# An attention layer's end rows joined in five groups of tiles, and duplicate edges counted against near keys only, in a four-network graph kernel on one core

## The reference

```python
edge_index = jnp.stack([src, dst])
x = _layernorm(x + _L0_gnn_ref(x, edge_index, W, att_src, att_dst, bias), axis=-1)   # attention, 8 heads
x = _layernorm(x + _L1_gnn_ref(x, edge_index, w0a, b0a, w0b, b0b, ...), axis=-1)     # 3 x sum of neighbours and two dense layers
x = _layernorm(x + _L2_gnn_ref(x, edge_index, W, att_src, att_dst, ...), axis=-1)    # attention, 4 heads, with a skip product
x = _layernorm(x + _L3_gnn_ref(x, edge_index, edge_weight, W1, b1, ...), axis=-1)    # 3 x weighted sum of neighbours
```

```python
alpha = leaky_relu(a_src[src] + a_dst[dst], 0.2)
alpha = exp(alpha - segment_max(alpha, dst)[dst])
out = segment_sum(x[src] * (alpha / (segment_sum(alpha, dst)[dst] + EPS))[:, :, None], dst)
```

## Time and profile before

| | |
|---|---|
| time of three runs, us | 7126.04 median (7118.27 to 7150.4) |
| time of the profiled execution, us | 7125.99 |
| its span, us | 7124.2 |
| DVE busy | 3269.2 us, 46% of the span |
| POOL busy | 3459.4 us, 49% |
| PE (TensorE) busy | 3212.4 us, 45% |
| first scatter (L593, `plane<-begun,cell`) | 782 instructions, 831.9 us busy, 338.9 us idle before them |
| duplicate count (L556) | 782 instructions, 756.8 us busy, 211.4 us idle before them |
| span of the first scatter | 1363.4 to 2533.9 us |

### The profile page before, as it was taken

The page is one execution under the profiler, slowest core; times in us unless marked ns, Lnnn a source line. Parts: engine busy times, 40 slices in busy tenths (PEclk is TensorE's granted clock), DMA queues, the critical chain, the costliest instruction groups (busy, mean ns, idle before and its releaser), DMA issues. The chain is left out here.

```text
span 7124.2 us, 38615 instructions
## 1 busy us (share of the span) xinstructions
PE 3212.4 (45%) x11661; PEld 2005.2 (28%) x11661; DVE 3269.2 (46%) x5638; ACT 1783.3 (25%) x1855; POOL 3459.4 (49%) x3338
## 2 busy tenths in 40 slices
PE   3000000000000079999999500000015999999999
PEld 2000000000000057777778400000013444544544
DVE  5565555698687723445657344444446000000111
ACT  1233333100000056666667322222210000000000
POOL 3677777677667755556667277777730000000000
PEclk8555555555555589999999755555557999999999
DMA  3355555209950056433358333333323888888887
GB/s 108 137 206 172 188 175 185 93 0 329 372 219 0 0 174 210 151 106 111 111 163 251 122 99 110 98 106 102 102 70 104 284 293 294 288 293 294 294 299 261
DMA packets 502441, 1242.14 MB, mean 174 GB/s; under 512 B 114227, under 2 KB 162841, under 8 KB 493273
## 3 DMA queue, kind: packets, MB, share of 16 engines
q1 hardware_dynamic: 382408, 1114.01, 45.8%
q0 software_dynamic: 119824, 125.65, 7.4%
HBM read 861.79 MB, written 377.50 MB: 174 GB/s over the span
## 5 line engine op out<-in xcount | busy, mean ns | idle before, releaser
L361 POOL DMA_INDIRECT gb<-rows,src x1564 | 1589.8, 1017 | 679.0 <-issue 548.5
L754 PE MATMUL psum<-gb,big 128*128 128x512 f32 (+1 forms) x3822 | 1579.3, 568 | 3.0 <-DVE gb L778 2.0
L593 POOL DMA_INDIRECT plane<-total,cell x782 | 836.4, 1070 | 558.0 <-DVE gb L574 192.9
L1108 ACT CAST strips<-gb 128x1024 fp32r<-128x1024 f16 (+1 forms) x764 | 805.1, 1077 | 1068.2 <-DMA gb<-plane 913.9
L1820 PE MATMUL psum<-identity,end_top 128*8 128x128 f32 (+1 forms) x2 | 0.8, 375 | 2277.6 <-issue 1173.9
L593 POOL DMA_INDIRECT plane<-begun,cell x782 | 831.9, 1064 | 338.9 <-issue 236.1
L1091 PE MATMUL psum<-strips,high 128*128 128x512 f32 (+1 forms) x1274 | 398.9, 401 | 1269.1 <-DVE strips L778 1252.9
L754 PEld LDWEIGHTS psum<-gb,big 128*128 128x128 f32 x3822 | 691.5, 190 | 770.9 <-issue 770.9
L556 DVE SCALAR_TENSOR_TENSOR psum<-gb,psum 128x782 f32<-128x782 f32 x782 | 756.8, 1032 | 211.4 <-remote 136.6
L1820 PEld LDWEIGHTS psum<-identity,end_top 128*8 128x8 f32 (+1 forms) x2 | 0.2, 82 | 2278.3 <-issue 1174.3
L1805 ACT COPY gb<-turned 128x1632 f32<-128x1632 f32 (+3 forms) x138 | 450.7, 3266 | 727.6 <-DVE turned L1893 514.6
(11 more groups left out here) (305 smaller groups left out, 3754.9 us busy)
## 6 DMA issues: line engine op xcount, KB each, us to landing
gb<-plane SPq DMA_DIRECT2D x588, 512.0 KB, 4.5
gb<-plane SPq DMA_DIRECT2D x294, 576.0 KB, 4.8
plane<-turned SPq DMA_DIRECT2D x49, 3200.0 KB
gb<-plane SPq DMA_DIRECT2D x588, 256.0 KB
gb<-plane SPq DMA_DIRECT2D x294, 288.0 KB
plane<-turned SPq DMA_DIRECT2D x49, 1600.0 KB
runs<-gb SPq DMA_DIRECT2D x33, 1748.0 KB
runs<-gb SPq DMA_DIRECT2D x33, 1610.0 KB
```

The costliest lines, as they stand in the source:

```text
L361: m.s_rows[b % BUFS].up(nc.gpsimd.indirect_dma_start(m.batch(b, columns, row)[:, j, 0:width], None, table, bass.IndirectOffsetOnAxis(ap=m. ...
L593: done.up(m.nc.gpsimd.indirect_dma_start(plane, bass.IndirectOffsetOnAxis(ap=m.cell[:, r:r + 1], axis=0), total[:, r:r + 1], None), 16)
L754: mm = nc.tensor.matmul(m.psum[:, self.bank(r, 0, i), 0:nodes], rows, slot[:, a:a + nodes], start=(s == 0), stop=False)
L1108: m.s_strip_act.up(nc.scalar.copy(out, landed))
```

## The change

Two parts.

**Near keys.** `count_edges` compares column `r` of group `b` with the first `near = min(COLS, (b + 3) * 23)` columns alone. The width of the instruction grows by 23 with every group, from 69 in group 0 to 782 from group 31 on. The number of instructions stays.

**Groups of end rows.** The 49 tiles are taken as 12, 12, 12, 12 and 1 (three quads, then what is left). DVE waits for the quads of one group, makes its factors, and then scales and adds the rows of the group before it; the last group's rows come at the end. ACT's two exponentials become five pairs.

```diff
@@ count_edges
+        near = min(COLS, (b + BUFS) * NARROW)
         for r in range(b * NARROW, (b + 1) * NARROW):
             if r > 1:
                 dve.wait_ge(m.s_compared.sem, r - 1)
             m.s_compared.up(nc.vector.scalar_tensor_tensor(
-                m.unread[r % 2], m.key, m.key[:, r:r + 1], m.step[:, COLS - 1 - r:2 * COLS - 1 - r], ALU.is_equal, ALU.mult,
+                m.unread[r % 2][:, 0:near], m.key[:, 0:near], m.key[:, r:r + 1], m.step[:, COLS - 1 - r:COLS - 1 - r + near], ALU.is_equal, ALU.mult,
                 accum_out=m.total[:, r:r + 1]))
+def end_groups():
+    return [slice(t, min(t + 3 * QUAD, TILES)) for t in range(0, TILES, 3 * QUAD)]
@@ attention_layer, ACT
-            act.wait_ge(m.s_logits.sem, m.s_logits.at(batches + 3))
-            m.s_probs.up(nc.scalar.activation(a, a, ACT.Exp))
-            m.s_probs.up(nc.scalar.activation(b_, b_, ACT.Exp))
+            for n, t in enumerate(end_groups()):
+                act.wait_ge(m.s_logits.sem, m.s_logits.at(batches + 3 + n))
+                m.s_probs.up(nc.scalar.activation(a[:, t, :], a[:, t, :], ACT.Exp))
+                m.s_probs.up(nc.scalar.activation(b_[:, t, :], b_[:, t, :], ACT.Exp))
@@ attention_layer, DVE
-            for g in range(QUADS):
-                dve.wait_ge(m.s_end[g].sem, m.s_end[g].at(16 * len(tiles_of(g))))
...
+            def factors(t):
+                node_top, own_top = ends[:, t, S:S + H], own[:, t, S:S + H]
+                for g in range(t.start // QUAD, -(-t.stop // QUAD)):
+                    dve.wait_ge(m.s_end[g].sem, m.s_end[g].at(16 * len(tiles_of(g))))
...
+            def add(n, t):
+                size = t.stop - t.start
+                many = [P, size, H, C + 1]
+                dve.wait_ge(m.s_probs.sem, m.s_probs.at(batches + 2 + 2 * (n + 1)))
...
+            groups = end_groups()
+            for n, t in enumerate(groups):
+                factors(t)
+                if n:
+                    add(n - 1, groups[n - 1])
...
+            add(len(groups) - 1, groups[-1])
```

More of the change, by code:

```diff
@@ L1934, in _ @@
                 count_edges(m, dve, 0, COUNTED_BEFORE)
-            for g in range(QUADS):
-                dve.wait_ge(m.s_end[g].sem, m.s_end[g].at(16 * len(tiles_of(g))))
+            def factors(t):
+                node_top, own_top = ends[:, t, S:S + H], own[:, t, S:S + H]
+                for g in range(t.start // QUAD, -(-t.stop // QUAD)):
+                    dve.wait_ge(m.s_end[g].sem, m.s_end[g].at(16 * len(tiles_of(g))))
+                c.link(nc.vector.tensor_tensor(own_top, node_top, b_[:, t, :], ALU.max))
+                c.link(nc.vector.tensor_tensor(a[:, t, :], node_top, own_top, ALU.subtract))
+                c.link(nc.vector.tensor_scalar(a[:, t, :], a[:, t, :], LOW, None, ALU.max))
+                m.s_logits.up(nc.vector.tensor_tensor(b_[:, t, :], b_[:, t, :], own_top, ALU.subtract))
@@ new lines, in add @@
+            def add(n, t):
+                size = t.stop - t.start
+                many = [P, size, H, C + 1]
+                dve.wait_ge(m.s_probs.sem, m.s_probs.at(batches + 2 + 2 * (n + 1)))
+                c.start(nc.vector.tensor_tensor(split(ends_sum[:, t, :]), split(ends_sum[:, t, :]),
+                                                a[:, t, :].unsqueeze(3).broadcast_to(many), ALU.mult))
+                c.link(nc.vector.tensor_tensor(split(own_sum[:, t, :]), split(own_sum[:, t, :]),
+                                               b_[:, t, :].unsqueeze(3).broadcast_to(many), ALU.mult))
+                c.link(nc.vector.tensor_tensor(own_sum[:, t, :], own_sum[:, t, :], ends_sum[:, t, :], ALU.add))
@@ L1937, in _ @@
+            groups = end_groups()
[3 more added lines that the diff above has]
+                    add(n - 1, groups[n - 1])
             if head.first:
                 c.start(nc.vector.tensor_scalar(m.dinv[:, :], ends[:, :, S + H], 1.0, None, ALU.add))
-            node_top = ends[:, :, S:S + H]
-            c.link(nc.vector.tensor_tensor(own[:, :, S:S + H], node_top, b_, ALU.max))
-            c.link(nc.vector.tensor_tensor(a, node_top, own[:, :, S:S + H], ALU.subtract))
@@ L1942, in _ @@
-            c.link(nc.vector.tensor_scalar(a, a, LOW, None, ALU.max))
-            m.s_logits.up(nc.vector.tensor_tensor(b_, b_, own[:, :, S:S + H], ALU.subtract))
-            dve.wait_ge(m.s_probs.sem, m.s_probs.at(batches + 4))
-            many = [P, TILES, H, C + 1]
-            c.link(nc.vector.tensor_tensor(split(ends_sum), split(ends_sum), a.unsqueeze(3).broadcast_to(many), ALU.mult))
-            c.link(nc.vector.tensor_tensor(split(own_sum), split(own_sum), b_.unsqueeze(3).broadcast_to(many), ALU.mult))
@@ L1948, in _ @@
-            c.link(nc.vector.tensor_tensor(own_sum, own_sum, ends_sum, ALU.add))
+            add(len(groups) - 1, groups[-1])
     m.settle()
```

## The result

The changed kernel takes 7100.29 us (median of 14 executions, 7089.84 to 7114.79), the kernel before 7117.34 (median of 14, 7086.16 to 7163.68). The ratio is 0.9965, its 95% interval 0.9951 to 0.9979: 25 us less, 14 to 35 by the interval. The gain is real, but smaller than the 0.5% that was named as the bound of no change. The forecast was 7009 in a range from 6988 to 7045, with a chance of 0.94 for more than 0.5%: wrong, since most of the gain it saw didn't come. The profiled executions show 7125.99 before and 7089.84 after, 36 us; the time is followed in these two.

The account below looks back on a forecast made before the run. The prediction took POOL's scatter to end the stage, with DVE counting only where POOL waits. It summed -16.8 - 94.2 - 6 = -117 against the profiled 7125.99 to 7009 us, range 6988 to 7045.

Parts of the forecast that it names:

- What bounds the kernel: First scatter's stage: POOL, not DVE, ends it; DVE counts only where POOL waits for it, 102.2 us in 12 waits.
- The start of group 2's scatter: First layer: POOL starts group 2's scatter at 1431.5 instead of 1448.3 without stopping, -16.8 us, including 7.98 of waiting.
- The second layer: Second attention layer's end: joining end rows in groups saves 10.3 us, gathers and factors cost 4.4; net -6 us.
- The waits behind it: From group 2's scatter on: POOL's remaining 94.2 us of waits for DVE's cells all go if DVE stays ahead.
- 23% of the counts stay at 2.8 us: DVE's groups 8 to 33: slow share stays 23% of 598 counts, so 724 us are needed, done at 2278.
- The worst bound: DVE's groups 8 to 33: rate unchanged at 1.51, then 1.34 us a count, done at 2400; POOL loses 6 us.
- a starved start: Rival, 14%: a slow stretch falls into group 2, some 16 counts at 2.8 us; POOL waits 33 us, time 7042.
- POOL's 1.27 us: First layer's scatter from group 2 on: POOL needs 1.27 us a scatter, 29.3 us a group, reaching the last group at 2394.
- The rival on the other side: Slower than before, 2%: DVE's supply of instructions bounds the counts; 40% slow counts gives the old end, 50% gives 7240.
- The place where I said I would look: DVE's slow stretches: instruction fetch not fully hidden may explain them, and blocks used up sooner could make them worse.
- The two that didn't: Slower than before, counts bound by DVE's instruction supply (2%, 7240 us); nothing gained, width doesn't set a count's cost (3%, 7120).

Follow-up runs that it names:

- before_again: The kernel before, unchanged, run and traced once more at the 7100 level: 7147.43 us (one execution; 7157.51 the median of 23 in this set).
- after_again: The whole change, unchanged, run and traced once more beside the kernel before at the 7100 level: 7131.91 us, ratio 0.9968.
- batched: The change with a group's 23 counts made in three DVE instructions over the keys of five groups: 7107.53 us, ratio 0.9947 of the kernel before.
- batched_fill_2: Three-instruction counts per group plus 200 unused DVE comparisons behind the last count, against the change: 7085.44 us at 7100; 6790.8 us, 0.9965, at 6815.
- one_more_4: The change with a one-column memset added to each count from group 2 on: 7142.7 us at 7100; 6793.43 (0.9968), 6793.51 and 6791.58 us at 6815.
- near_only: The kernel before with near keys and no groups of end rows, at the 6815 level: 6807.37, 6804.61 and 6807.53 us, ratios 0.9989, 0.9986, 0.9989.
- groups_only: The change with full-width counts put back, so groups of end rows alone, at the 6815 level: 6801.18 and 6800.3 us, ratio 0.998 in both.

## Why the prediction was wrong, point by point

**What bounds the kernel: right.** POOL's scatter ends the stage in both kernels, and its end moved SP's load with it.

**The start of group 2's scatter, -16.8: right.** It measured -14.6 (1433.76, forecast 1431.5), with no wait. The joins of 1.85 us beside the scatters cost POOL a little more than one scatter of 1.85 for each. The scatters took 2.65, 1.45 and 1.58 us beside the first three, and the gathers ahead ended 6.2 us later than before.

**The second layer, -6: right**, at -5.8. The part at the end measured 11.1 us (25.6 to 14.5), forecast 10.3; the gathers paid 5.3, forecast 4.4. Beside a join's three instructions of 1.80 us the timeline has gathers of 2.49, 1.41 and 1.54 us in place of 0.95. The lock between DVE and POOL of which the Trainium skill's page "SBUF — State Buffer", section "SBUF: two separate sides", speaks is there; but one POOL instruction passes for each of DVE's, as the forecast took it from the rows.

**The waits behind it, -94.2: this is the step that failed.** It measured -6.9; in the second pair of traces, before_again and after_again, it was -1.2 (17.3 us at group 2's start, 18.5 at the last scatter). In the prediction's words, "They go if DVE stays ahead", and "both ends of this unknown leave at least 88 of the 94.2, and I take all of it". Three things in that step were wrong.

1. *23% of the counts stay at 2.8 us.* The share of slow counts was read as a property that would carry over. It depends on POOL's waits: a slow stretch lasts until POOL stops, and POOL stops when it has used up DVE's lead. With faster counts between the stretches the lead is larger, POOL takes longer to use it up, and the stretch goes on for more counts. So 17, 17, 18, 17, 29, 17 and 9 counts a stretch became 38, 37, 39, 24, 23, 24 and 23 in the first pair of traces. DVE's pace from group 8 on went from 32.5 us a group to 31.3, and in the second pair from 32.3 to 32.8. What the faster counts gained between the stretches was given back in them. What begins a stretch, no run shows.
2. *The worst bound.* It had this very case, "its rate stays what it was", at 1.51 and 1.34 us a count. The rate was 1.41 for groups 8 to 20 and 1.31 behind them, near the bound. But the bound was started from a lead of 91 us, with group 7 done at 1554. A slow stretch of 94 us (1439.1 to 1532.7) lay in groups 4 and 5, so group 7 came at 1633.5. The rival "a starved start" had this, but at 16 counts and with fast counts behind it. Each was priced as if the other didn't occur, though both are the same mechanism. Together they are 6 + 80 = 86 us lost, 7009 + 86 = 7095; 7100 was measured. That this comes so close is partly luck. The bound compares only the ends, and there DVE was ahead: its last cells came at 2447, and POOL began that group at 2483. What POOL lost it lost in the waits on the way.
3. *POOL's 1.27 us.* The prediction took POOL's pitch as free of everything once the waits were gone. At 7100 POOL comes down to 1.40 in the two kernels without waits, some 290 us behind the SELU stage's wide instructions (batched, batched_fill_2). So even with all waits gone POOL takes 1050 us from group 2's first scatter (1433.9) to the last (2484.1), where the forecast had 991. The term was too large by 59 us even for a kernel that does what the change was to do.

**From the scatter's end to the second layer's end rows, forecast 0**: this part brought 8.4 us in the profiled pair. In the second pair it lost 4.8 (a lead of 18.5 us became 13.7), so it differs from execution to execution and isn't a gain of the change as far as these traces show.

**The rival on the other side** ("the counts are bound by DVE's supply of instructions", 2%) named the right mechanism, with the point at 40% slow counts. 181 of 736 are 25%. That POOL's waits cap the share is the reading that fits these traces. one_more_4 shows the rival's direction: with one instruction more for each count the waits grow to 129.5 us.

**The place where I said I would look.** The Trainium skill, "Runtime: NRT & Kernel Launch", "Instruction fetch mechanics", lets an engine's next block of instructions arrive by DMA while the present one is executed, mostly hidden. The trace agrees only in part. In after_again, an instruction packet appears at 1452, and from 1455 to 1520, in the middle of the slow stretch from 1440.9 to 1525.7, there is none:

```profile
DMA packets 1632, 0.02 MB, mean 0 GB/s; under 512 B 1632, under 2 KB 1632, under 8 KB 1632
## 3 DMA queue, kind: packets, MB, share of 16 engines
q0 software_dynamic: 1632, 0.02, 1.9%
```

The only queue in that stretch is POOL's scatter. So the slow counts aren't a wait for one block on its way; DVE goes on, in steps of 0.70 us. Where that pace arises, and what POOL's DMA issuing has to do with it, stays open: that the instructions are what comes late is inferred from the count of instructions (one_more_4, batched), not seen. It also stays open what differs at 6815, and what the parts alone, near_only and groups_only, bring at 7100, where they never ran.

**The chances.** 0.94 for more than 0.5% stood on cases that all let most of the 94 us go. The two that didn't had 5% together, although the case with an unchanged rate was in the text as a bound. A cost that "no operation of the program explains" is one whose law isn't known, and it should have kept a third of the chance.

The fastest kernel of the study at 7100 by more than one execution is batched (0.9947 of before; the change 0.9968 in the same set), at 6815 batched_fill (0.9965), level with one_more (0.9968).

## What to carry to other kernels

Idle time that nothing in the program explains has to be given a law before the instructions around it are made shorter: if it goes by instructions, as the 2.80 us of a slow count did at 7100, a shorter instruction gains nothing there, and one more costs 0.70 us. Compare the time that the same piece of work takes (here 31.3 us a group for 32.5), not its busy time (down by a quarter); where the first hardly moves, the width wasn't the bound. And two cases that come from the same mechanism are to be priced together, from the state in which the first leaves the kernel.

## What the runs showed of the hardware

- At 7100, beside indirect DMAs that POOL issues without a pause, DVE goes through stretches of 10 to 150 us in which a count starts 2.80 us after the one before (median), be it 1.04 or 0.53 us long, and 3.50 with a memset of 0.06 us added. In the first pair of traces they end 4 to 12 us after POOL begins to wait; six of ten pauses by memsets of 8.2 us in all ended one too. Instructions of 2.91 us, three a group, show nothing of it.
- At 7100 POOL without waits keeps up 1.27 us an indirect DMA for some 290 us, then 1.40 (0.97 and 1.10 us of its own work), with DVE idle or busy; 1.40 is twice 0.70, which may or may not mean something.
- In each of the eight traces at 7100, 86 to 95 distances of POOL's 1564 gathers (L361) are 2.10 or 2.80 us, in place of 1.25; at 6815 at most 2 are.
- At 6815 none of the twelve traces has a slow stretch, and in the nine that have the scatter POOL keeps 1.27 us from group 8 to the end.
